# Moving the routing steps of the second attention one row tile later

## The reference, cut to what matters

```python
# x: (B=4, S=1024, D=128)
Q, K, V = x @ WQ.T, x @ WK.T, x @ WV.T
W = Q @ K.T / sqrt(D)                       # per batch, 1024 x 1024
x_exp = exp(W - max(W, -1)) * where(W == 0, 0, tril)
x = x + x_exp / (sum(x_exp, -1) + 1e-9) @ V
n = (x - mean) / sqrt(var + 1e-5)
logits = n @ gate_w + gate_b                # 16 experts
top_probs, top_idx = top_k(softmax(logits), 2)
dispatch = top_probs / sum(top_probs)       # then the experts' layers, weighted by dispatch
```

## Time and profile before

| what | value |
|---|---|
| median of 3 runs | 1975.84 us (1970.2 to 1978.46) |
| span of the profiled execution | 1999.1 us |
| the profiled execution's own time beside the span | none is given; the span is 23.3 us over the median |
| mean granted TensorE clock | 0.910 |
| busy over the span: TensorE, VectorE, ScalarE, GpSimd | 83%, 67%, 50%, 15% |

### The profile page before, as it was taken

The page is one execution under the profiler, slowest core; times in us unless marked ns, Lnnn a source line. Parts: engine busy times, 40 slices in busy tenths (PEclk is TensorE's granted clock), DMA queues, the critical chain, the costliest instruction groups (busy, mean ns, idle before and its releaser), DMA issues. The chain is left out here.

```text
span 1999.1 us, 29912 instructions
## 1 busy us (share of the span) xinstructions
PE 1666.4 (83%) x9244; PEld 864.8 (43%) x9244; DVE 1334.0 (67%) x2664; ACT 1004.8 (50%) x1883; POOL 293.4 (15%) x300
## 2 busy tenths in 40 slices
PE   4999598799999998589776169945999999996998
PEld 2767344122222223475554158832222222225676
DVE  4753589888888866346766224446888888856566
ACT  2555233276766775014433146634377777675343
POOL 1010200101100011100023535550000110011000
PEclk9999799699999998699987579967699999997899
DMA  2260039024454410104000132137423223300001
GB/s 82 97 143 6 18 111 225 25 34 81 78 91 76 72 45 14 24 5 129 5 18 22 37 93 77 41 102 196 100 50 60 54 54 54 54 15 22 0 0 42
DMA packets 116627, 122.70 MB, mean 61 GB/s; under 512 B 24203, under 2 KB 90355, under 8 KB 115495
## 3 DMA queue, kind: packets, MB, share of 16 engines
q1 hardware_dynamic: 101118, 102.13, 22.6%
q0 software_dynamic: 15408, 19.31, 3.4%
HBM read 79.06 MB, written 41.84 MB: 60 GB/s over the span
## 5 line engine op out<-in xcount | busy, mean ns | idle before, releaser
L1037 DVE TENSOR_REDUCE heads_mx<-scales_n_bank 128x1 f32<-128x1024 f32 (+2 forms) x280 | 324.4, 1196 | 61.3 <-PE scales_n_bank L903 59.7
L1037 DVE TENSOR_REDUCE heads_mx<-edge_n_bank 128x1 f32<-128x1024 f32 x256 | 301.6, 1219 | 52.0 <-PE edge_n_bank L903 50.6
L1018 ACT ACTIVATE heads_prob<-scales_t_bank 128x512 f32<-128x512 f32 x512 | 264.5, 603 | 139.9 <-PE scales_t_bank L922 139.9
L1018 ACT ACTIVATE heads_prob<-edge_t_bank 128x512 f32<-128x512 f32 x512 | 264.5, 603 | 134.4 <-PE edge_t_bank L922 134.4
L903 PE MATMUL scales_n_bank<-scale_ks,scale_qs 96*128 96x512 bf16 (+2 forms) x608 | 177.4, 383 | 27.4 <-DVE heads_mx L1037 14.1
L903 PE MATMUL edge_n_bank<-edge_ks,edge_qs 99*128 99x512 bf16 x512 | 164.6, 406 | 24.5 <-PEq L43 13.5
L922 PE MATMUL scales_t_bank<-scale_qs,scale_ks 99*128 99x512 bf16 (+2 forms) x608 | 170.1, 368 | 3.5 <-ACT heads_prob L1018 3.5
L922 PE MATMUL edge_t_bank<-edge_qs,edge_ks 102*128 102x512 bf16 x512 | 155.5, 383 | 3.5 <-ACT heads_prob L1018 3.5
L938 PE MATMUL edge_o_bank<-heads_prob,edge_vs 128*32 128x512 f32 x1024 | 136.4, 605 | 0.1
L938 PE MATMUL scales_o_bank<-heads_prob,scale_vs 128*32 128x512 f32 x1024 | 136.4, 605 | 0.0
L903 PEld LDWEIGHTS scales_n_bank<-scale_ks,scale_qs 96*128 96x128 bf16 (+1 forms) x608 | 46.7, 101 | 176.2 <-issue 99.8
(11 more groups left out here) (362 smaller groups left out, 2690.1 us busy)
## 6 DMA issues: line engine op xcount, KB each, us to landing
edges_text<-edges_targets SPq DMA_DIRECT2D x16, 512.0 KB, 3.6
scale_qs<-scale_q_parts SPq DMA_DIRECT2D x60, 128.0 KB, 4.9
scale_ks<-scale_k_parts SPq DMA_DIRECT2D x60, 128.0 KB, 6.9
heads_wide<-heads_inverse_d POOLq DMA_DIRECT2D x15, 512.0 KB, 9.6
edge_qs<-edge_q_parts SPq DMA_DIRECT2D x48, 128.0 KB
edge_ks<-edge_k_parts SPq DMA_DIRECT2D x48, 128.0 KB
routed_x<-attn_zeros SPq DMA_DIRECT2D x2, 2600.0 KB
experts_xs<-routed_x SPq DMA_DIRECT2D x16, 325.0 KB
```

The source lines that it names most:

```text
L1018: act.activation(to[:], t_ps[score_bank(of, place, g)[0]][0:TN, 0:HP * CH], ACT.Exp, scale=scale).then_inc(exped, 1)
L1037: dve.tensor_reduce(mx[:, u % UC:u % UC + G], scores, AX.X, ALU.max, negate=True).then_inc(first_used, 1)
```

## The change

The routing steps of the preceding batch move one row tile later in the three loops. On TensorE `turn_rows(f, 0)` goes from t = 1 to 2, `turn_rows(f, 1)` from 3 to 4, `gate_logits` from 4 to 5 and `count_picks` from 6 to 7. On ScalarE `take_rows` goes from 2 and 3 to 3 and 4, `double`, `take_odds` and `arm` from 4, 5 and 6 to 5, 6 and 7; `take_root` stays at t = 0; the eight `normalise` instructions stood as 2, 2 and 4 in t = 0, 1 and 2, and stand as 4 and 4 in t = 1 and 2. On VectorE `find_shift`, `choose`, `pick` and `hand_out` go from 0, 4, 5 and 6 to 1, 5, 6 and 7; `place_rows(f)` goes from t = 7 of batch f + 1 to t = 0 of batch f + 2, but for the last one that has attention beside it, `place_rows(2)`, which stays in tile 31. No step is added or left out.

```diff
-            inside = {3: lambda f: turn_rows(f, 1), 4: gate_logits, 6: count_picks}
+            inside = {4: lambda f: turn_rows(f, 1), 5: gate_logits, 7: count_picks}
...
-                if b >= 1 and t == 1:
+                if b >= 1 and t == 2:
                     turn_rows(b - 1, 0)
...
-                if b >= 1 and t == 2:
+                if b >= 1 and t == 3:
                     take_rows(f, 0)
...
-                if b >= 1 and t == 3:
+                if b >= 1 and t == 4:
                     take_rows(f, 1)
...
                 if b >= 1 and t == 0:
                     take_root(f)
-                    normalise(f, 0, 2)
                 elif b >= 1 and t == 1:
-                    normalise(f, 2, 4)
+                    normalise(f, 0, 4)
                 elif b >= 1 and t == 2:
                     normalise(f, 4, 8)
-                elif b >= 1 and t == 4:
+                elif b >= 1 and t == 5:
                     double(f)
-                elif b >= 1 and t == 5:
+                elif b >= 1 and t == 6:
                     take_odds(f)
-                elif b >= 1 and t == 6:
+                elif b >= 1 and t == 7:
                     arm(f)
...
-            beside = {0: (find_shift,), 4: (choose,), 5: (pick,), 6: (hand_out,), 7: (place_rows,)}
+            beside = {1: (find_shift,), 5: (choose,), 6: (pick,), 7: (hand_out,)}
+            in_order = (find_shift, choose, pick, hand_out, place_rows)
...
                 if b >= 1:
                     for part in beside.get(t, ()):
                         part(b - 1)
+                if b == B - 1 and t == T - 1:
+                    place_rows(b - 1)
+                elif b >= 2 and t == 0:
+                    place_rows(b - 2)
                 if b >= 2 and t == 1:
                     note_pages(b - 2)
             measure(B * T - 1)
             note_pages(B - 2)
-            for parts in beside.values():
-                for part in parts:
-                    part(B - 1)
+            for part in in_order:
+                part(B - 1)
             note_pages(B - 1)
```

## The result

Four runs of the changed kernel have a median of 1961.32 us (1958.34 to 1967.17), four of the kernel before 1973.26 (1970.2 to 1978.46). The ratio is 0.9944, with a 95% interval of 0.9926 to 0.9963: **11.9 us faster**, where 11.3 were forecast. The forecast time, 1964.5 us, lies 3.2 above it, 2.6 of which come from the kernel before, whose median was 1975.84 when the forecast was made. The profiled execution after took 1967.17 us at a span of 1965.3.

A forecast was written before the change was run, and what follows sets the result against it. A chain through several engines, none full, was taken as the bound, with VectorE bounding a batch's second half. Gains 4.8 + 1.9 + 2.5 + 1.9 + 1.5 − 1.3 = 11.3 took 1975.84 to 1964.5 us, range 1955 to 1974.

The forecast's parts named there:

- its first step: Batch 1, tiles t = 1 and 2: keep_turned(9) directly behind the root, turn(10) 4.65 us earlier, 4.8 gained at turn(12).
- Tiles t = 1 and 2: First tiles of batch 1: turn_rows leaves tile 9, a smaller stall moves to mix in tile 10; 4.8 us gained.
- Tiles t = 4 to 0: Tiles 12 to 16, again 20 to 24: VectorE's chain from choose loses place_rows, gains one tile; 1.9 us gained each.
- Batch 3: No projection fills the wait behind the four normalises, place_rows(1) stands in tile 24; 1.5 us gained, between 0 and 3.4.
- the tail: Behind mix(31), hand_out(2) delays measure(31) and GpSimd's third burst by 2.56 us, 1.2 paid back by pick; 1.3 us lost.
- TensorE's wait for normalise: Sign of being right: this wait within the attention falls from 17.2 us to about 10.
- The hold: Some 14 us after a batch's first scatter engines see signals late; it moves to tiles 20 and 21 at price 0.
- both rivals built on it: The hold grows, 11 us more for each of two, 1986, chance 0.07; the hold costs less, 1957, chance 0.18.
- The stall only moves: Rival: four normalises hold keep_turned of tile t = 2 as long as turn_rows held TensorE; 1972 us, chance 0.23.
- The drain: Rival: first copy behind the root comes a further 1.4 us late in each of three batches; 1968.5 us, chance 0.02.

The follow-up runs named there:

- the first profile: The kernel before, unchanged, as profiled for the forecast: span 1999.1 us, turn(8) to GpSimd's last burst 188.19 us.
- the second profile: The kernel before, unchanged, profiled once more: 1970.04 us, span 1968.2, turn(8) to GpSimd's last burst 163.21 us.
- Experiment 4: Against the kernel before, only turn_rows(f, 0) and take_rows(f, 0) one tile later: 1963.78 us, ratio 0.9946.
- experiment 2: Against the kernel before, only the front half (find_shift, normalise, turn_rows(f, 0), take_rows(f, 0)) one tile later: 1959.65 us, ratio 0.9923.
- experiment 3: Against the kernel before, only the back half, turn_rows(f, 1) to hand_out one tile later, place_rows moved as in the change: 1976.15 us, ratio 1.0012.
- experiment 5: Against the changed kernel, place_rows back in tile t = 7 for all batches: 1965.04 us, ratio 0.9953 to the kernel before.
- experiment 7: Against the changed kernel, batch 3 with the back half placed as in the kernel before: 1959.99 us, ratio 0.9922 to the kernel before.

## Why the prediction was right

The sum was right, and so was its first step; how it divides between the two halves of the change was not. The gain at each point, from the table above:

| up to | forecast | against the first profile | against the second |
|---|---|---|---|
| turn(12) | 4.8 | 4.93 | 6.47 |
| mask(17) | 6.7 | 6.93 | 8.47 |
| turn(19) | 9.2 | 9.66 | 9.40 |
| mask(25) | 11.1 | – | 11.55 |
| turn(28) | 12.6 | – | 12.49 |
| b4 | 11.3 | – | 12.01 |

- *Tiles t = 1 and 2.* Right, and for the reason given. Every position up to turn(19) came within 0.6 us of the forecast, once turn(8)'s 9.75 us are taken off (954.90 after, 945.15 in the first profile). Against the second profile the gain comes sooner (6.47 by turn(12)), because there scores(12) fell to the lower clock level behind the 2.54 us of idling (3.62 us). In the first profile it didn't fall as far:

```profile
957.19 2.54 PE L2012 MATMUL attn_s_bank<-attn_k,attn_q 128*128 128x512 f32 x4
```

  By turn(19) the two are the same. So the close match at each point is with the execution that the forecast was worked out from. Experiment 4 shows that `turn_rows` in tile 1 was most of it.
- *Tiles t = 4 to 0.* Up to the masks the size was right: 2.0 and 2.2 us for 1.9 each, turn(12) to mask(17) from 25.30 to 23.30 and turn(19) to mask(25) from 31.73 to 29.58. But most of it is lost again behind them. Against experiment 2, the front half alone, the whole change is 2.3 us ahead at mask(17), 0.9 at turn(19), 3.0 at mask(25) and 0.8 at b4; and in experiment 3 the back half alone has the same gain before mask(17) and loses it by turn(19). With the front half, place_rows at t = 0 is worth 3.5 us (experiment 5), part of it by the clock (an estimated 2.27 of turn(18)'s 3.0), which the prediction didn't have; the other steps of the back half take 2.7 of that back (152.02 to 154.73).
- *The split, and luck.* The front half's terms are 4.8, 2.5 and, with all of batch 3's, 1.5, so 8.8 at most; it gave 11.2 alone. The back half's are 1.9, 1.9 and −1.3, so 2.5; it gave 0.8 on top and nothing alone. That the sum came within 0.7 us of 12.0 is in part these two errors cancelling.
- *Batch 3* was 1.5 and measured 0.9 (mask(25) to turn(28), 18.27 to 17.33); *the tail* was −1.3 and measured −0.5 (turn(28) to b4, 48.69 to 49.17). Both terms were mis-sized, in opposite directions. In the tail the wait for batch 3's normalises did grow by 2.6 (7.9 to 10.5), as hand_out's 2.56 says, and is 7.9 again in experiment 7. pick's 1.2 came back as 1.3 (turn(28) to turn(31), 15.83 to 14.51); but from turn(31) to b4 only 1.8 were lost (32.86 to 34.66), not 2.56.
- *TensorE's wait for normalise* was to fall to about 10 and came to 12.7, by those same 2.6, which that sentence left out.
- *The hold.* Taken as a property of the kernel, at a price of 0 for its move. It was none: both rivals built on it, with 0.25 of the chance, spoke of something that is absent from nine other profiles. That the engines saw signals late was not shown either; the rows have the idle times alone. The price of 0 kept the error out of the sum. That the span stood 23.3 us over the median, about the 25.0 that the holds cost, was the sign, and the prediction named the figure without drawing the conclusion.
- *The stall only moves* falls: mix(10) waits 0.95 us where more than 4 were asked for. The largest wait of this kind is in batch 3, before mix(26), timeline of TensorE after:

```profile
1050.79 1.65 PE L2034 MATMUL attn_o_bank<-attn_v,attn_probT 128*128 128x128 f32 x6 [2.31 <-ACT attn_probT L2110]
```

  *The drain* falls too: keep_turned(9) starts 0.21 us after the root's start, and the root 0.02 after the table load's end. The Trainium skill, "ScalarE: Activation LUTs", section "What ACT_TABLE_LOAD costs", states a further drain at each switch to a different set; neither the trace before nor the one after shows it, and the trace decides.
- *Two sums are off by little.* 1009.93 less 1000.8 is 9.1, not 9.2, and three times 1.4 on 1964.5 is 1968.7, not 1968.5; neither changes the argument.

Of the six kernels that move turn_rows(f, 0), the two with the longer stages (154.5 and 154.7) have the higher medians (1963.8 and 1965.0); the other four (stages of 149.2 to 152.0) can't be told apart by theirs (1959.6 to 1961.3), as the ten runs of the change alone lie between 1955.96 and 1967.17.

## What to carry to other kernels

Where a step beside a pipeline wants a result made in the same tile, moving its consumer one tile on can be worth more than the wait that the trace names. Part of that can be the clock: in the first stretch here it went from 0.93 to 1.00 and took 3.3 us off TensorE's work (41.70 to 38.44). Try the step that the wait names first, and alone: here turn_rows with its copy gave 8.7 of 12 us. Try each half of a change that has two, too: the sum of a forecast can be right while its terms are not. And before a stall of a profile is taken as the kernel's, set the span against the median: when it is longer by as much as the stalls sum to, they may belong to that execution.

## What was not expected of the hardware

- Stalls of 5.21 us on VectorE, for nothing that the profile shows, and 5.86 us on TensorE, in one execution of ten profiled; with their like behind the next two bursts the stage took 25.0 us more. Their cause wasn't found.
- How much a short idle time costs behind it: after 1.27 us the granted clock was 0.97, after 4.08 it was 0.54 (experiment 5); and the same 2.54 us of idling in the kernel before were followed by scores(12) of 2.54 us in one execution and 3.62 in the other. Nor does the idle time before it settle the level: after 2.52 us before turn(17), scores(19) took 3.16 us in experiment 2 and 1.88 in experiment 4. What else does, no run here shows.
- Positions within the stage repeat within 0.12 us between two executions of the change, but up to turn(19) only within 1.6 between the two of the kernel before, by the clock of a few matmuls (scores(12) alone 1.1), while the stage's own start moves by up to 9.8 us between kernels that do the same ahead of it.
